# Attention stage of a decoder layer: transposed scores in single banks, exponentials of 512 columns, and a ring of four banks for the maxima

## The reference, cut to what matters

```python
qkv = x @ W_qkv + b_qkv                      # x normalised, 4 x 1024 x 768
q, k, v = split and reshape to 4 x 1024 x 16 heads x 16
energy = jnp.einsum('bqhe,bkhe->bqhk', q, k)
attn = jax.nn.softmax(energy, axis=-1) / sqrt(E)
out = jnp.einsum('bihv,bvhd->bihd', attn, v)
return out.reshape(B, N, E) @ W_out + b_out
```

## Time and profile before

| | us |
|---|---|
| median of 3 runs | 1218.48 (1216.84 to 1220.51) |
| the profiled execution's own time | 1215.71 |
| its span, first to last instruction | 1213.6 |
| TensorE busy | 1148.9 (95%) |
| VectorE busy | 1048.5 (86%) |
| ScalarE busy | 832.4 (69%) |
| GpSimd busy | 293.3 (24%) |

### The profile page before, as it was taken

The page is one execution under the profiler, slowest core; times in us unless marked ns, Lnnn a source line. Parts: engine busy times, 40 slices in busy tenths (PEclk is TensorE's granted clock), DMA queues, the critical chain, the costliest instruction groups (busy, mean ns, idle before and its releaser), DMA issues.

```text
span 1213.6 us, 18448 instructions
## 1 busy us (share of the span) xinstructions
PE 1148.9 (95%) x6476; PEld 584.9 (48%) x6476; DVE 1048.5 (86%) x1974; ACT 832.4 (69%) x1386; POOL 293.3 (24%) x403
## 2 busy tenths in 40 slices
PE   6999999999999999999999999997899999999995
PEld 4544333333333333333333333333467778767775
DVE  5688799999999999999999999985799899898875
ACT  4321577777787777777777777774778777778852
POOL 2124010110110111011011000013565456545421
PEclk9999899999999999999999999999999999999998
DMA  5877112650330431332133100024111121000001
GB/s 171 251 217 243 53 36 34 142 112 16 62 59 6 63 58 24 45 58 41 29 61 55 18 11 6 6 69 109 55 35 39 52 70 48 24 18 18 1 18 36
DMA packets 45916, 74.95 MB, mean 62 GB/s; under 512 B 10112, under 2 KB 23808, under 8 KB 45824
## 3 DMA queue, kind: packets, MB, share of 16 engines
q0 software_dynamic: 9648, 27.27, 13.2%
q1 hardware_dynamic: 36176, 46.50, 12.8%
HBM read 47.53 MB, written 25.69 MB: 60 GB/s over the span
## 4 chain that ended last, share of the span: by engine, by line
PE 75%; DVE 16%; ACT 3%; issue 3%; POOL 1%; DMA 1%; SPq 1%; DVEq 0%; ACTq 0%; POOLq 0%
PE ps L1242 21%; PE ps L1361 20%; PE ps L1205 15%; DVE maxes L849 10%; PE ps L1520 4%; PE ps L1440 4%; PE ps L1347 3%; PE ps L1505 2%; PE ps L1449 2%; ACT prob L619 1%; ACT pe_ L688 1%; PE ps L1459 1%; DVE xhat L1100 1%; DVE maxes L842 1%; PE ps L1409 1%
## 5 line engine op out<-in xcount | busy, mean ns | idle before, releaser
L849 DVE TENSOR_REDUCE maxes<-ps 128x1 f32<-128x512 f32 x968 | 608.6, 683 | 55.1 <-PE ps L1242 55.1
L619 ACT ACTIVATE prob<-ps 128x1024 f32<-128x1024 f32 x512 | 495.7, 1021 | 149.1 <-PE ps L1347 146.1
L1242 PE MATMUL ps<-Ks,Qs 48*128 48x512 f32 x1024 | 363.5, 475 | 17.8 <-DVE maxes L842 2.6
L1242 PEld LDWEIGHTS ps<-Ks,Qs 48*128 48x128 f32 x1024 | 143.1, 184 | 359.7 <-DVE maxes L849 323.5
L1361 PE MATMUL ps<-prob,V_all 128*32 128x512 f32 x2048 | 273.6, 606 | 0.7 <-ACT prob L619 0.7
L1347 PE MATMUL ps<-Qs,Ks 50*128 50x512 f32 x1024 | 238.1, 411 | 3.3 <-DVE parts L874 2.1
L330 POOL DMA_DIRECT2D Qs<-qk_scratch x90 | 44.4, 500 | 486.1 <-PE ps L1361 486.0
L1347 PEld LDWEIGHTS ps<-Qs,Ks 50*128 50x128 f32 x1024 | 133.9, 186 | 19.5 <-ACT prob L619 11.6
L688 ACT ACTIVATE pe_<-ps,nmx 128x64 f32<-128x64 f32 x512 | 109.4, 376 | 7.2 <-DVE nmx L1019 7.1
L539 POOL TENSOR_TENSOR pe_<-pe_,rsum 128x512 f32<-128x512 f32 x64 | 66.6, 1050 | 55.6 <-DVE rsum L1036 55.6
L1520 PE MATMUL ps<-t_p,fT 128*128 128x256 f32 x512 | 77.8, 295 | 0.0
(11 more groups left out here) (115 smaller groups left out, 1232.1 us busy)
## 6 DMA issues: line engine op xcount, KB each, us to landing
qk_scratch<-parts SPq DMA_DIRECT2D x32, 512.0 KB, 5.3
Qs<-qk_scratch POOLq DMA_DIRECT2D x90, 128.0 KB, 5.3
Ks<-qk_scratch POOLq DMA_DIRECT2D x90, 128.0 KB, 7.8
o_scratch<-ot SPq DMA_DIRECT2D x128, 32.0 KB
on_raw<-o_scratch SPq DMA_DIRECT2D x8, 512.0 KB
r_raw<-r_scratch SPq DMA_DIRECT2D x16, 256.0 KB
x_in<-in_x SPq DMA_DIRECT2D x8, 512.0 KB, 4.0
out<-xo SPq DMA_DIRECT2D x8, 512.0 KB, 2.8
```

The costliest lines, as they stand in the source:

```text
L619: act.activation(prob[:, par, h].rearrange("p a q -> p (a q)"), ps[:, 2 * h:2 * h + 2, :].rearrange("p a q -> p (a q)"), ACT.Exp).then_inc ...
L849: dve.tensor_reduce(maxes[:, qc, j * BLK + blk, half:half + 1], ps[:, MAX_BANK["tile", t], :], AX.X, ALU.max).then_inc(max_reduced, 1)
L1242: pe.matmul(ps[:, bank, :], stack(Qs[g], j, STACK, slice(q0, q0 + P)), stack(Ks[g], j, STACK, slice(half * 512, (half + 1) * 512)), start= ...
```

## The change

Banks 0, 1 and 2 become a ring for single scores: score n of the whole stage (four per unit) goes to bank n % 3, and its exponential takes 512 columns. The heads come in the order 1, 0, 3, 2. Bank 3 joins the ring of the maxima, which then has banks 3, 5, 6 and 7, and a use waits for the one four earlier. A score waits for the exponential three before it. On TensorE the four scores of U + 1 stand singly between the maximum tiles, the last one behind `values(U)`; on ScalarE the copy to `ot` comes ahead of the last exponential of U + 1.

```diff
+ST_HEADS = (1, 0, 3, 2)
+ST_BANKS = 3
+
+MAX_BANKS = (3, 5, 6, 7)
...
-MAX_BANK = {use: 5 + n % 3 for n, use in enumerate(MAX_RING)}
+MAX_BANK = {use: MAX_BANKS[n % 4] for n, use in enumerate(MAX_RING)}
 MAX_BANK["rows", 0] = 2
-MAX_BEFORE = {use: MAX_RING[n - 3] for n, use in enumerate(MAX_RING) if n >= 3}
+MAX_BEFORE = {use: MAX_RING[n - 4] for n, use in enumerate(MAX_RING) if n >= 4}
...
-            def exps(U, par):
-
-                for h in range(2):
-                    act.wait_ge(st_done, 2 * U + h + 1)
-                    act.activation(prob[:, par, h].rearrange("p a q -> p (a q)"),
-                                   ps[:, 2 * h:2 * h + 2, :].rearrange("p a q -> p (a q)"),
-                                   ACT.Exp).then_inc(exp_done, 1)
+            def exps(U, lo, hi):
+
+                for n in range(4 * U + lo, 4 * U + hi):
+                    j = ST_HEADS[n % 4]
+                    act.wait_ge(st_done, n + 1)
+                    act.activation(prob[:, U % 2, j // 2, j % 2, :], ps[:, n % ST_BANKS, :], ACT.Exp).then_inc(exp_done, 1)
...
-            exps(0, 0)
+            exps(0, 0, 4)
...
                     act.wait_ge(pv_done, U)
-                    exps(U + 1, (U + 1) % 2)
+                    exps(U + 1, 0, 3)
                 if U % KB == KB - 1:
                     act.wait_ge(pv_done, U + 1)
                     act.wait_ge(o_written, O_WRITES * (U // KB))
                     act.activation(ot[:], ps[:, 4, :], ACT.Copy).then_inc(o_copied, 1)
+                if U + 1 < GROUPS * UNITS:
+                    exps(U + 1, 3, 4)
...
-            def scores(U, h):
+            def scores(U, k):
...
-                if U:
-                    pe.wait_ge(exp_done, 2 * U + h - 1)
-                for j in ((1, 0), (2, 3))[h]:
-                    i = pe.matmul(ps[:, j, :], stack(Ks[g], j, ROWS, slice(kb * P, (kb + 1) * P)),
-                                  stack(Qs[g], j, ROWS, slice(qc * CH, (qc + 1) * CH)), start=True, stop=True)
-                i.then_inc(st_done, 1)
+                if n >= ST_BANKS:
+                    pe.wait_ge(exp_done, n - ST_BANKS + 1)
+                pe.matmul(ps[:, n % ST_BANKS, :], stack(Ks[g], j, ROWS, slice(kb * P, (kb + 1) * P)),
+                          stack(Qs[g], j, ROWS, slice(qc * CH, (qc + 1) * CH)), start=True, stop=True).then_inc(st_done, 1)
...
-                pe.wait_ge(exp_done, 2 * U + 2)
+                pe.wait_ge(exp_done, 4 * U + 4)
...
-            scores(0, 0)
-            scores(0, 1)
+            for k in range(4):
+                scores(0, k)
...
                 scores(U + 1, 1)
                 max_tile(t + 2)
+                scores(U + 1, 2)
                 values(U)
                 if LAST_ROWS < U <= LAST_ROWS + 4:
                     prepare(U - LAST_ROWS - 1)
+                scores(U + 1, 3)
                 max_tile(t + 3)
```

More of the change, by code:

```diff
@@ L1341, in scores @@
                 g, (qc, kb) = group % NG, divmod(s, KB)
-                if kb == 0 and h == 0:
+                n, j = 4 * U + k, ST_HEADS[k]
+                if kb == 0 and k == 0:
                     pe.wait_ge(m_loaded, 16 * HG * (U // KB + 1))
-                if U:
-                    pe.wait_ge(exp_done, 2 * U + h - 1)
-                for j in ((1, 0), (2, 3))[h]:
-                    i = pe.matmul(ps[:, j, :], stack(Ks[g], j, ROWS, slice(kb * P, (kb + 1) * P)),
-                                  stack(Qs[g], j, ROWS, slice(qc * CH, (qc + 1) * CH)), start=True, stop=True)
-                i.then_inc(st_done, 1)
+                if n >= ST_BANKS:
+                    pe.wait_ge(exp_done, n - ST_BANKS + 1)
+                pe.matmul(ps[:, n % ST_BANKS, :], stack(Ks[g], j, ROWS, slice(kb * P, (kb + 1) * P)),
+                          stack(Qs[g], j, ROWS, slice(qc * CH, (qc + 1) * CH)), start=True, stop=True).then_inc(st_done, 1)
             def values(U):
```

## The result

Over 19 executions each, the changed kernel took 1217.03 us (median) and the kernel before 1217.94; the ratio is 0.9956, 95% interval 0.9934 to 0.9977. By that ratio it is 5.4 us faster, where 12.9 us had been forecast. The two medians themselves lie only 0.9 us apart, for the reason that follows.

The account below looks back on a forecast made before the run. The prediction took a loop through TensorE and VectorE, 2.70 us a unit, to bound the kernel. Its terms, -23.7 + 2.8 + 8 = -12.9 us, took the 1218.5 us median to 1205.6 us, range 1194 to 1224.

Parts of the forecast that it names:

- The units with tiles: Attention units that have maximum tiles: a gain of 0.79 us per eight units, -23.7 us over 30 such stretches.
- The loop: Last exponential, score 2, values, score 3, last exponential, once in each unit: 2.62 us against 2.70.
- Eight units: Attention stage, transpose to transpose: 8 x 2.62 plus 0.10 for the copy to `ot`, 21.06 us against 21.85.
- abs_part: Four activations on ScalarE, each now ahead of exponential 0: 0.7 us each, +2.8 us.
- The waits: Attention stage: hardly any TensorE loads waiting for reductions; ScalarE waiting once a unit, some 0.4 us, for score 3.
- The exponential of 512: ScalarE's 128x512 exponential: 0.60 us, taken from the copy to `ot` of same shape and types (0.598).
- The units without tiles: From unit 243 on: 2.62 us instead of 2.06, +6.7 us, with +1.3 for products of `prepare`: +8 us.
- `prepare` in full: 1.93 us of products put three times into the new cycle, where some 0.4 each was hidden before: +1.3 us.
- Rival 3: Slower: TensorE's clock falls to 1.2 GHz in the attention stage; repeated stretches give above 1230 us; repeated case's chance 0.05.
- smaller form: Several half-clock stretches, some 3 us each, at the attention stage's end: 1210 to 1215 us; no separate chance.
- The sum: Whole kernel: -23.7 + 2.8 + 8 = -12.9 us, from a median of 1218.5 to 1205.6 us.
- -20.9: Attention stage up to unit 243: -23.7 us for the 30 stretches, with +2.8 us for the four activations.

Follow-up runs that it names:

- half filler: Changed kernel plus two products a unit that nobody reads on TensorE in units 243 to 254: 1206.48 us, ratio 0.9881.
- mended schedule: Changed kernel, but from unit 244 scores use four banks and score 3 is issued ahead of the previous unit's values: 1197.38 us, ratio 0.9796.

## Why the prediction was wrong

**The units with tiles: right.** The loop was to be 2.62 us and is 2.60 to 2.61. Eight units were to take 21.06 us; the transposes around `abs_part` lie 64.7 us apart for three stretches (next paragraph), and the other 26 take (612.8 - 64.7) / 26 = 21.08. The waits are where they were said to be. The exponential of 512, taken at 0.60 from the copy, is 0.600.

By the figure that the prediction took from the Trainium skill (ScalarE: Activation LUTs, Rules for kernel authors) the exponential would take 0.72 us, an estimate. That figure is for an instruction whose bias is a pointer, and the kernel gives this one no bias; with one, L607 took 0.687 us. So the prediction's remark that the rows don't agree with its constant held two different forms against each other, and the 0.600 here says nothing against it.

**abs_part: oversized.** +2.8 forecast. The transposes around it in the changed kernel's trace, four of them, start between 292.0 and 356.7 us: 64.7 us, less 3 x 21.08 is 1.5. Why the stall is half of what was reckoned was not tested.

**The units without tiles: the step that failed, by its clock.** The term of +8 us (2.62 instead of 2.06 for twelve units, and `prepare` in full) is right at full clock: with the half filler the transpose of unit 243 is again at 775.6 and the last copy at 815.1, 39.5 us against 31.4, so +8.1. But the sum took a granted clock of 1.00 for these units without saying so, and that is the step that failed: the same units took 50.6 us in the profiled execution, 34.2 us of them at 0.50, which is 11.1 more, and behind them came two stretches of 3.4 us at half clock (+2). Only one execution was profiled; that the other thirteen of 1215 us and more went the same way is inferred from their mean clock: 34.2 us at half clock take 0.014 off the mean, which is the step from 0.991 to 0.977. For the two at 0.987 and 0.988 this is open.

Clock and loop multiply: the loop holds 0.43 + 0.99 + 0.50 us of TensorE's work in series, and these grow to 0.79 + 1.86 + 0.77 when the clock falls, so that a step goes from 2.61 to 4.07.

**Rival 3** was the one that came, in its smaller form ("Several in the stage's end give 1210 to 1215"). That form had no chance of its own, and it was priced too low: one stretch of 34 us and not several of some 7, and 1217.9 us for the median of the fourteen. The prediction had even worked out that TensorE would idle some 0.7 us of 2.62 there, where it had been above 90% occupied, and did not draw the consequence. The Trainium skill (TensorE: Matmul & The Clock Gate, A second HAM failure mode: psum-queue depth-cycling) warns of a clock that alternates with short idles while banks are cycled. The runs don't bear out the banks as the cause: the same ring kept 1.00 for 640 us with tiles, and the kernel before fell to 0.50 with its own banks once it had such a loop. Short idles alone don't bring the fall either, as the 636 us at 1.00 with three banks for the maxima show, and it stayed at 0.50 instead of alternating. What the runs show is narrower: in the last units of the stage the clock fell, in most executions, where the loop had neither tiles nor filler beside it, and it stayed up where filler stood beside the loop or the loop was gone. How much waiting it takes stays open.

**The sum, told again with measured terms:** -19.1 up to unit 243 (the stage began 1.5 us later: 10.3 us at half clock there instead of 6.8), +8.1 for the loop, +11.1 for the clock in these units, +2 behind them. Without the last two: -11.0, which gives 1204.7, near the three executions at 1204. The prediction had -20.9 where -19.1 came: the stage began 1.5 us later, and the last of the 30 stretches isn't one of eight units: it runs over units 236 to 242, and 242 has no tiles. It took 18.4 us (757.2 to 775.6) where the kernel before took 18.1 (776.6 to 794.7), so it gained nothing. The smaller stall of `abs_part` gave 1.3 back.

## What to carry to other kernels

When a change removes a wait from the steady state, follow the new loop also into the iterations that have less work in them: a loop that is a gain beside the maximum tiles costs 0.55 us a unit (2.61 against 2.06) where there are none. And if TensorE is left waiting there, price these iterations at both clocks; in the profiled execution and, by their times, in thirteen more, 12 units out of 256 took back the gain of the others. The cure was a schedule of their own for them (0.9796 of the kernel before, against 0.9956), and a few useless products were a cheap test of the cause.

Banks go together: the split of the exponentials was worth 0, single scores with three banks for the maxima +1.7%, both with the fourth bank -0.4%, and -2.0% with the last units mended. The second and third of these contain losses to the clock.

## What the runs showed that was not expected

- Useless work made the kernel faster: 24 unread products, 0.24 us each, brought the ratio to the kernel before from 0.9956 to 0.9881 (the medians, 1217.0 and 1206.5 us, come from separate measurements).
- A low clock can last although TensorE seems occupied: with score 2 behind the values, in one execution, it had records for 61.14 of 61.4 us at 1.2 GHz, right at the stage's start, and the records don't show why it fell or why it rose in the end:

```profile
128.40:189.80 61.40, 61.14 (x218) 24.83 (x216) 32.59 (x58) 29.64 (x59) 0.00 (x0) 0.50 0.05 15
```

- The same program shows both outcomes, 1204 and 1217 us, from one execution to the next. What decides between them was not found. Of eleven executions with filler (1203.3 to 1208.3 us) and four with the mended schedule (1195.1 to 1199.4), none came near 1215.
